# The low parts of a token tile's four query heads and its key head, computed by one VectorE instruction instead of two

## The reference

```python
q = (x @ Wq + bq).reshape(b, s, NQ, D)
k = (x @ Wk + bk).reshape(b, s, NKV, D)
q = _rotary(q)
k = _rotary(k)
qg = q.reshape(b, s, NKV, g, D)
logits = jnp.einsum('bqhgd,bkhd->bhgqk', qg, k) * scale
logits = jnp.where(causal, logits, jnp.float32(-1e+30))
w = jax.nn.softmax(logits, axis=-1)
out = jnp.einsum('bhgqk,bkhd->bqhgd', w, v).reshape(b, s, NQ * D)
```

## Time and profile before

| | |
|---|---|
| Median of 3 runs | 1169.94 us (1166.63 to 1174.44) |
| The profiled execution | 1168.11 us, of which the trace spans 1166.6 us |
| Mean granted TensorE clock | 0.979 of full speed |
| PE busy | 1086.5 us, 93% |
| DVE busy | 851.2 us, 73% |
| POOL busy | 588.1 us, 50% |
| ACT busy | 549.4 us, 47% |

### The profile page before, as it was taken

How to read it: one execution, slowest core, us unless ns; L and a number is a source line. 1 busy time by engine, 2 the same in 40 slices (tenths; PEclk the granted TensorE clock), 3 DMA queues, 4 the chain that set the end, 5 groups by cost and what they waited for, 6 DMA issues and landing times.

```text
span 1166.6 us, 16696 instructions
## 1 busy us (share of the span) xinstructions
PE 1086.5 (93%) x5727; PEld 656.0 (56%) x5727; DVE 851.2 (73%) x1754; ACT 549.4 (47%) x1155; POOL 588.1 (50%) x633
## 2 busy tenths in 40 slices
PE   3789999999999999999999999999999989888993
PEld 2456565554565555545555655455556455477892
DVE  5777978777778787677888786777787879764333
ACT  2444544545455445454545454544454344653451
POOL 5544655646346557364354673545455624626441
PEclk8899999999999999999999999999999999999997
DMA  8000000000000000000000000000020002332104
GB/s 229 20 1 1 1 1 1 1 1 1 1 1 1 1 1 1 1 1 1 1 1 1 1 1 1 1 1 1 1 72 1 1 1 78 90 82 83 32 24 122
DMA packets 30018, 25.08 MB, mean 22 GB/s; under 512 B 4480, under 2 KB 25344, under 8 KB 29936
## 3 DMA queue, kind: packets, MB, share of 16 engines
q1 hardware_dynamic: 26224, 18.45, 5.8%
q0 software_dynamic: 2272, 4.72, 1.2%
q10 hardware_dynamic: 1440, 0.85, 0.2%
HBM read 15.62 MB, written 8.40 MB: 21 GB/s over the span
## 4 chain that ended last, share of the span: by engine, by line
PE 71%; DVE 13%; issue 6%; POOL 5%; DMA 2%; ACT 1%; ACTq 0%; SPq 0%; DVEq 0%; POOLq 0%
PE PS L1535 18%; PE PS L1483 12%; PE PS L1517 11%; PE PS L1519 9%; PE PS L1619 3%; DVE part_max L1109 3%; PE PS L1458 3%; PE PS L1496 2%; POOL sent L760 2%; PE PS L1585 2%; PE PS L1643 2%; PE PS L1465 2%; PE PS L1559 2%; DVE full L1127 2%; PE PS L1486 1%
## 5 line engine op out<-in xcount | busy, mean ns | idle before, releaser
L1109 DVE TENSOR_REDUCE part_max<-PS 128x1 f32<-128x512 f32 (+2 forms) x576 | 339.7, 618 | 123.2 <-PE PS L1483 100.2
L875 ACT ACTIVATE full<-PS 128x512 f32<-128x512 f32 x384 | 222.7, 599 | 197.8 <-PE PS L1519 186.7
L1517 PE MATMUL PS<-store 128*128 128x512 f32 (+3 forms) x640 | 272.8, 426 | 2.0 <-ACT full L875 1.2
L1483 PE MATMUL PS<-store 128*128 128x512 f32 (+3 forms) x640 | 250.4, 417 | 9.7 <-ACT store L855 4.0
L1519 PE MATMUL PS<-store 128*128 128x512 f32 (+3 forms) x640 | 234.7, 367 | 0.0
L713 POOL TENSOR_TENSOR full<-full 128x512 f32<-128x512 f32 x120 | 155.6, 1328 | 136.9 <-PE PS L1535 135.8
L884 ACT ACTIVATE diag<-PS 128x512 f32<-128x512 f32 (+3 forms) x256 | 111.5, 441 | 207.8 <-PE PS L1522 173.3
L1483 PEld LDWEIGHTS PS<-store 128*128 128x128 f32 x640 | 119.1, 191 | 145.0 <-DVE part_max L1109 62.4
L1535 PE MATMUL PS<-full,V 128*64 128x512 f32 x768 | 190.9, 607 | 0.0
L743 POOL TENSOR_TENSOR lower<-lower 128x320 f32<-128x320 f32 x64 | 60.1, 939 | 255.7 <-DVE lower L1087 253.6
L1517 PEld LDWEIGHTS PS<-store 128*128 128x128 f32 x640 | 123.7, 193 | 72.8 <-ACT diag L884 21.0
(11 more groups left out here) (227 smaller groups left out, 1492.4 us busy)
## 6 DMA issues: line engine op xcount, KB each, us to landing
lower<-in_L_ffn_experts_w_dram SPq DMA_DIRECT2D x16, 256.0 KB, 4.1
sent<-full SPq DMA_DIRECT2D x1, 2574.0 KB, 12.5
full<-sent SPq DMA_DIRECT2D x9, 264.0 KB, 3.9
lower<-made SPq DMA_DIRECT2D x8, 256.0 KB, 5.2
full<-in_L_attn_x_dram SPq DMA_DIRECT2D x2, 512.0 KB, 7.6
out_dram<-XA SPq DMA_DIRECT2D x4, 256.0 KB, 2.7
made<-lower,back_to POOLq DMA_INDIRECT x39, 2.2
wo_sb<-in_L_attn_Wo_dram SPq DMA_DIRECT2D x1, 512.0 KB, 11.1
```

Of the source, the lines that this page charges most:

```text
L875: nc.scalar.activation(full[:, k % QUADS, r, :], PS[:, bank, :], ACT.Exp).then_inc(probs_ready, 1)
L1109: nc.vector.reduce_max(part_max[:, t, b:b + 1], PS[:, bank, 0:width], AX.X).then_inc(ring_dve, 1)
L1483: last = nc.tensor.matmul(PS[:, bank, 0:w], QT(ch % 2, h, t * P, (t + 1) * P), keys[:, 0], start=True, stop=not last_bank)
L1517: nc.tensor.matmul(o, keys[:, 0], QT(ch % 2, h, q0, BANK), start=True, stop=False)
```

## The change

The two areas `q_split` and `k_split` become one, `split`, with 769 words per tile: 5 heads (4 queries and the key) of a high and a low half each, then one word that holds 1.0, then the key's high part twice. `halves_of(b)` gives the 5 heads of tile b.

- ScalarE's first copy rounds all 5 heads (320 columns instead of 256); the second copy still writes the key twice, now behind the word 1.0; the third stays.
- VectorE subtracts all 5 heads in one instruction of 320 columns. The second instruction, of 64 columns, is gone.
- TensorE transposes as many pieces as before, from other offsets. The second key piece is the window [key low, 1.0, the first 63 words of the key's high part]. Where zeros stood there are now key numbers; the matmul's other operand still has zeros in those rows.
- One GpSimd memset at the start (63 zero columns for 4 tiles) goes.
- A tile's row begins at 769 words times its number in the chunk, and all that stands behind `split` in `store`, and behind `store` in memory, is 4 words further on.

```diff
-        QMAX_W, QS_W, KS_W = 2 * TB * QH * P, TB * QH * 2 * HEAD, TB * 2 * P
-        store = sb("store", [P, KS_W + QMAX_W + QS_W + 6 * HALF_W + KEY_SLOTS * SLOT_W], F32R)
+        QMAX_W, SPLIT_W = 2 * TB * QH * P, TB * (2 * QK + 1 + P)
+        store = sb("store", [P, SPLIT_W + QMAX_W + 6 * HALF_W + KEY_SLOTS * SLOT_W], F32R)
...
-        q_split = area["q_split"].rearrange("p (t h a n) -> p t h a n", t=TB, h=QH, a=2)
-        k_split = area["k_split"].rearrange("p (t a n) -> p t a n", t=TB, a=2)
+        split = area["split"].rearrange("p (t n) -> p t n", t=TB)
+
+        def halves_of(b):
+
+            return split[:, b, 0:2 * QK].rearrange("p (h a n) -> p h a n", a=2, n=HEAD)
...
-            nc.gpsimd.memset(k_split[:, :, 1, HEAD:HEAD + 1].bitcast(F32), 1.0)
-            nc.gpsimd.memset(k_split[:, :, 1, HEAD + 1:P].bitcast(F32), 0.0)
+            nc.gpsimd.memset(split[:, :, 2 * QK:2 * QK + 1].bitcast(F32), 1.0)
...
-                nc.scalar.copy(q_split[:, b, :, 0, :], q)
-                nc.scalar.copy(k_split[:, b, 0, :].rearrange("p (a n) -> p a n", a=2), k).then_inc(parts_ready, 1)
+                nc.scalar.copy(halves_of(b)[:, :, 0, :], rotated[:, b % 2].rearrange("p (h n) -> p h n", n=HEAD))
+                nc.scalar.copy(split[:, b, 2 * QK + 1:2 * QK + 1 + P].rearrange("p (a n) -> p a n", a=2), k).then_inc(parts_ready, 1)
...
-                    nc.vector.tensor_tensor(q_split[:, b, :, 1, :],
-                                            rotated[:, b % 2, 0:QH * HEAD].rearrange("p (h n) -> p h n", n=HEAD),
-                                            q_split[:, b, :, 0, :].bitcast(F32), ALU.subtract)
-                    nc.vector.tensor_tensor(k_split[:, b, 1, 0:HEAD], rotated[:, b % 2, QH * HEAD:QK],
-                                            k_split[:, b, 0, 0:HEAD].bitcast(F32), ALU.subtract).then_inc(low_ready, 1)
+                    nc.vector.tensor_tensor(halves_of(b)[:, :, 1, :], rotated[:, b % 2].rearrange("p (h n) -> p h n", n=HEAD),
+                                            halves_of(b)[:, :, 0, :].bitcast(F32), ALU.subtract).then_inc(low_ready, 1)
...
-                                                   q_split[:, i % TB, h].rearrange("p a b -> p (a b)").bitcast(F32),
+                                                   split[:, i % TB, 2 * h * HEAD:2 * (h + 1) * HEAD].bitcast(F32),
...
-                    for m in range(2):
-                        last = nc.tensor.transpose(PS[:, bank, m * P:(m + 1) * P], k_split[:, i % TB, m].bitcast(F32),
+                    for m, at in ((0, 2 * QK + 1), (1, 2 * QK - HEAD)):
+                        last = nc.tensor.transpose(PS[:, bank, m * P:(m + 1) * P], split[:, i % TB, at:at + P].bitcast(F32),
```

More of the change, by code:

```diff
@@ L373, in block_kernel @@
         HALF_W, SLOT_W = PAIRS * BANK, 2 * BANK
-        QMAX_W, QS_W, KS_W = 2 * TB * QH * P, TB * QH * 2 * HEAD, TB * 2 * P
-        store = sb("store", [P, KS_W + QMAX_W + QS_W + 6 * HALF_W + KEY_SLOTS * SLOT_W], F32R)
+        QMAX_W, SPLIT_W = 2 * TB * QH * P, TB * (2 * QK + 1 + P)
+        store = sb("store", [P, SPLIT_W + QMAX_W + 6 * HALF_W + KEY_SLOTS * SLOT_W], F32R)
         area, area_at = {}, {}
         at = 0
-        for name, words in (("k_split", KS_W), ("q_max", QMAX_W), ("q_split", QS_W), ("QT_even", 2 * HALF_W), ("QT_odd", HALF_W),
+        for name, words in (("split", SPLIT_W), ("q_max", QMAX_W), ("QT_even", 2 * HALF_W), ("QT_odd", HALF_W),
                             ("QMT", HALF_W), ("KT_free", SLOT_W), ("QT_odd_last", HALF_W), ("QMT_last", HALF_W),
```

## The result

| | before | after |
|---|---|---|
| Median | 1172.07 us (7 runs, 1166.63 to 1174.44) | 1166.10 us (7 runs, 1162.45 to 1167.16) |
| Ratio to before | | 0.9947, 95% interval 0.9925 to 0.9970 |
| The profiled execution | 1168.11 us, span 1166.6 | 1163.18 us, span 1161.6 |

Two more sets of runs of the same changed kernel, each beside runs of the kernel before, gave 1164.83 us and a ratio of 0.9933 (0.9912 to 0.9955), and 1163.67 us and 0.9929 (0.9915 to 0.9944). The change makes the kernel 0.5 to 0.7% faster, 6 to 8 us: the forecast was 0.4%, 4.7 us.

The account below looks back on a forecast made before the run. TensorE, busy for 93% of the span, was taken as the bound. 5.23 us off the chain less 0.21, 0.25 and 0.07 gave 4.7 us: 1163.4 us profiled, 1165.2 us as median, range 1158.5 to 1172 us.

Parts of the forecast that it names:

- The seam: Between VectorE's two subtractions GpSimd slips in, so the small one waits, then takes its 0.2 us; merged mean about 750 ns.
- Only nine places count: Low parts stand on the chain five times in the opening and once per group; 5.23 us leaves there, elsewhere hidden.
- The four groups, forecast 2.74 us: One chain place per attention group: gains of 3 x 0.70 + 0.64 us instead of 2.95 us.
- the cap: In each group the 0.74 us gain is limited to TensorE's idle 0.70 us (0.64 in the last), 0.21 us less.
- The opening, forecast 1.96 us: Five chain places before the attention: second pieces of 2.63 us, each replaced by 0.07 us; TensorE's waits there cut nothing.
- The two charges: In the opening, ScalarE's longer first copy costs 0.25 us (five times) and GpSimd's longer wait 0.07 us (once).
- nothing is gained: Rival: GpSimd's turn comes behind the merged subtraction and stalls the next two-SBUF-input VectorE instruction; 1169.9 us, chance 0.17.
- the forecast's own case: At the wait near 80 us more than 2 us of TensorE idle stays; with or without the clock's 1.5 us, chance 0.67.
- VectorE's busy time: Over the whole kernel it falls by 35 us, from 851 to 816 us, mostly hidden under TensorE.
- Slower by odd offsets: Rival: TensorE's six transposes per tile read slower at odd-word offsets; 1181.6 us at 43 ns each, chance 0.07.
- More than the chain shows: Rival: VectorE's 35 us also removes other TensorE idle time, bound 14.0 us, 1155.9 us; chance 0.09.
- The clock gives more: Rival: the shorter wait near 80 us avoids the low clock behind it, 1163.7 us; counted within the 0.67.

Follow-up runs that it names:

- e5_one_input: Changed kernel with two instructions again, the second a reduction of 63 zero columns with one SBUF operand, key's low part left zero: 1166.53 us, ratio 0.9951.
- e1_two: Changed kernel with the subtraction cut in two again at every tile (4 heads, then the key): 1173.27 us, ratio 1.0023.
- e4_five: Changed kernel with the subtraction cut into five of 64 columns, one per head: 1202.83 us, ratio 1.0272 to the kernel before.
- e3_not_nine: Changed kernel with the subtraction split again at the nine low steps on the chain, merged at the other 55 tiles: 1170.69 us, ratio 0.9996.
- e2_only_13: Changed kernel, split again except at four tiles, the second tile of each group's fourth chunk: 1169.29 us, ratio 0.9976.
- e9_before_moved: Kernel before, two subtractions kept, with pair 0's row sums and tile 8's low parts moved behind the maxima awaited near 80 us: 1167.56 us, ratio 0.9967.
- e6_moved: Changed kernel with pair 0's row sums, tile 8's low parts and three groups' output steps moved behind row maxima: 1161.82 us, ratio 0.9921.

## Why the prediction was right, point by point

**The seam.** Right, and shown. e5_one_input and the two sets of durations in before's own trace (210 to 219 ns without GpSimd beside it, 536 to 1,335 ns with it) show that the small subtraction's excess is the wait for GpSimd, and e1_two that without the merge there is no gain. One detail was read too simply: the subtraction doesn't start its 0.2 us when GpSimd's record ends. At 129 us the two end 0.08 us apart, in e4_five 0.08 to 0.09 us. The mean of the merged instruction is 723 ns (forecast 750, range 700 to 800), its least 475 ns (forecast 482).

**Only nine places count.** Right, and shown for the four groups: with merging at four tiles a group is 0.74 us shorter, with merging at 55 others 0.09 us.

**The four groups, forecast 2.74 us.** Mis-sized by some 0.7 us: 4 x 0.87 = 3.5 us. The step that failed is the cap, which took TensorE's idle time of 0.70 us for all that could be gained at the place. The recorded wait shrank by 0.53 us only (0.70 to 0.17, where less than 0.1 was forecast), so VectorE still comes last there, and the place gained 0.74 us: its matmuls start 1.98 us earlier than before ahead of it (128.04 against 130.02) and 2.72 us earlier at the wait (132.26 against 134.98). The rest comes from a wait that no bracket shows, 3 to 4 us earlier. The rows before, and then after:

```profile
130.43 0.86 PE L1458 MATMUL PS<-lower 128*128 128x384 f32 x2
131.22 0.51 PE L1483 MATMUL PS<-store 128*128 128x512 f32 x1
131.56 0.23 PE L1486 MATMUL PS<-causal,ident 128*128 128x128 bf16 x1
```

```profile
128.45 0.86 PE L1457 MATMUL PS<-lower 128*128 128x384 f32 x2
128.85 0.69 PE L1482 MATMUL PS<-store 128*128 128x512 f32 x1
129.39 0.23 PE L1485 MATMUL PS<-causal,ident 128*128 128x128 bf16 x1
```

Before, the maxima score matmul L1483 starts 0.79 us after the pair ahead of it, now 0.40 us. Its buffer comes free with the row maximum that stands behind the low parts: before, this ends at 131.16 us and L1483 starts at 131.22. Both rows ahead of it show 0.86 us, since the ends of matmuls are modelled, and this covered the 0.39 us. One row later, at L1486, 0.20 us of it is left (131.56 - 129.39 = 2.17 us, less the 1.98), and 0.20 + 0.53 us is what the place gained. VectorE's own rows say it more simply: from the low parts to step `maxed` it never waits for another engine, 5.70 us before (129.00 to 134.70) and 4.97 us after (127.01 to 131.98). The other 0.1 us of the 0.87 comes from the rest of the tiles (e3_not_nine).

**The opening, forecast 1.96 us** (2.63 less the 0.67 of charges). The first matmul to the long wait takes 69.7 us on average over the three traces of the changed kernel. In the four traces with a split opening and the long wait in place (before, e1_two, e2_only_13, e3_not_nine) it takes 72.2 us. That is 2.5 us less, with differences of 1.5 to 2 us within each set, so the term is of the right size and no more can be said. The two charges (0.25 us for ScalarE's copy, 0.07 us for GpSimd) are too small for any run here to test.

At the first of the five places another step failed: that a merged subtraction leaves no stall behind it. It had been read at 129 us, where row maxima follow, and taken for all nine places. At the very first tile an instruction with two operands in SBUF comes next but one. Before, and then after:

```profile
25.18 0.42 DVE L1003 SCALAR_TENSOR_TENSOR full<-gates 128x256 f32<-128x256 f32 x1
```

```profile
22.92 0.77 DVE L1005 SCALAR_TENSOR_TENSOR full<-gates 128x256 f32<-128x256 f32 x1
```

It takes 0.77 to 0.78 us in the six traces with a merged first tile and 0.42 to 0.43 us in the six where the tile is split. From the start of the low parts to the instruction behind this one it was 1.89 us (23.75 to 25.64) and is 1.79 us (21.94 to 23.73): the place gained 0.10 us, and the forecast had 0.47. This is the rival "nothing is gained", on the chain, at one of the nine places.

One pair of traces would have misled about the opening. Before's profiled execution had a late start that the change doesn't touch, which shows at its projection:

```profile
17.10 2.17 PE L1458 MATMUL PS<-lower 128*128 128x384 f32 x6 [1.17 <-DVE lower L1026]
```

This row comes 17.10 - 8.42 = 8.7 us after the first matmul, with a wait of 1.17 us. In every other trace of this study, e9_before_moved with its old layout among them, it comes after 7.2 to 7.9 us and without a wait. The first transposes of low parts come 16.5 us after the first matmul in this trace, and 14.6 to 15.3 us in the other four with a pair of subtractions there (e1_two, e2_only_13, e3_not_nine, e9_before_moved). So of the 2.3 us by which these transposes are earlier in the changed kernel's trace than in before's (22.61 against 24.87), more than 1 us is this late start.

**TensorE's wait near 80 us** fell to 2.32 us (forecast 2.3), and the stretch at the lower clock behind it stayed in all three traces, as the forecast's own case said. ScalarE's first copy takes 459 ns (forecast 450).

**VectorE's busy time** fell by 25.6 us, not 35. The low parts alone take 43.8 + 39.2 - 46.3 = 36.7 us less. Of the 11 us between the two, some 8 us are overlaps of neighbouring records, which the busy time counts once (5 us of it the 0.08 us of each pair L1095 and L1098), and some 3 us went into other instructions that take longer now. The largest of their groups, first of before and then of after:

```profile
L1154 DVE TENSOR_TENSOR full<-full 128x512 f32<-128x512 f32 x92 | 72.1, 788 | 0.0
```

```profile
L1153 DVE TENSOR_TENSOR full<-full 128x512 f32<-128x512 f32 x92 | 73.4, 802 | 0.0
```

It fits the stall moving on to the next instruction with two operands in SBUF, as the rival "nothing is gained" had it, but at 14 ns on average. Only for the first tile is it shown to fall on the chain.

**The sum.** Groups 3.5 and opening 2.5 give 6.0 us, against 4.7 forecast and 6 to 8 us measured. The rest, up to 2 us, stays open: it is within what the medians of the sets differ by. That the time of 1165.2 us came within 0.9 us of the measured 1166.10 is in part luck: the median before was 2.1 us lower at 3 runs (1169.94) than at 7 (1172.07), the gain was forecast 1.3 us too small, and the two errors have opposite signs. The two profiled executions differ by 4.9 us, near the 4.7, but more than 1 us of that is the late start.

**The rivals.** Slower by odd offsets: not seen, 279 ns before and after, e1_two's group is as long as before's, and the merged subtraction's least is 475 ns. More than the chain shows: not seen in the attention; the tiles off the chain are worth 0.1 us a group (e3_not_nine). Nothing is gained: so at the first tile only. The clock gives more: not so with a wait of 2.32 us.

## What to carry to other kernels

Where a short VectorE instruction with two operands in SBUF costs several times its least duration, look at what GpSimd does at its start: the price is the seam, and joining it to its neighbour, or giving it one operand in SBUF only, takes it away. Then look at the next instructions behind it: if one of them has two operands in SBUF, the stall can move there. It is worth time only where the chain of waits runs through it; here that was 9 of 64 places, and 20 us of VectorE's time elsewhere were worth 0.1 us a group. Read what a place gains from the distance between starts of the same instruction in two traces, since the idle time in brackets can hide a wait under a modelled end.

## What the runs showed of the hardware

- Beside a GpSimd instruction a 64-column subtraction with two operands in SBUF took 536 to 1,335 ns (40 cases), without one 210 to 219 ns (24 cases); an addition with one of its operands in PSUM took 473 to 493 ns in both cases, and a reduction with one operand 203 to 214 ns.
- Two engines that contend in trains of instructions take turns: five subtractions of 0.22 us took 4.06 us, each ending 0.08 to 0.09 us behind one of GpSimd's.
- In the attention seams don't add up linearly: one seam per tile makes a group 0.84 us longer (e1_two against after), three more make it 9.85 us longer (e4_five against e1_two). About a third of that is the clock, by the estimate above: the wait of 2.35 us was followed by 3.4 us at a granted clock of 0.53. Not every such wait is: one of 2.15 us in e4_five and three of 1.97 to 1.98 us in e6_moved were followed by no low stretch.
- A wait that is cut from 2.32 to 0.69 us gave back the low stretch behind it as well (in all four traces with 0.68 or 0.69 us), which a cut from 2.92 to 2.32 didn't (in all three).
